# Attention over token means: the sums from ScalarE's accumulator and a row spread from DRAM instead of matrix products, with earlier weighing of the adjacency

## What is computed

```python
fea = jnp.transpose(x, (0, 2, 1))
c_adj = jnp.mean(fea, axis=1)                       # one mean for each token
diff = c_adj[:, None, :] - c_adj[:, :, None]
A = jnp.abs(jnp.abs(jax.nn.sigmoid(diff) - 0.5) - 0.5) * 2.0
A_s = (A + jnp.transpose(A, (0, 2, 1))) * 0.5
Wg = adj[None, :, :] * A_s
g = jnp.einsum('bcn,bnm->bcm', fea, Wg)
g = jax.nn.relu(g * para.reshape(1, C, N))          # the queries, 4 heads
kv = (x @ kv_w)                                     # keys and values
attn = softmax(q k^T * scale); out = attn v         # for each head
x = layernorm(x + out)
```

## Time and profile before

| | |
|---|---|
| median of 3 runs | 3213.74 us (3212.96 to 3216.64) |
| profiled execution | 3214.61 us |
| its span, first to last instruction | 3212.8 us |
| mean granted TensorE clock | 0.968 of full speed |
| busy in the span | TensorE 2929.7, VectorE 2127.5, ScalarE 1674.4, GpSimd 1066.9 us |

### The profile page before, as it was taken

The page is one execution under the profiler, slowest core; times in us unless marked ns, Lnnn a source line. Parts: engine busy times, 40 slices in busy tenths (PEclk is TensorE's granted clock), DMA queues, the critical chain, the costliest instruction groups (busy, mean ns, idle before and its releaser), DMA issues. The chain is left out here.

```text
span 3212.8 us, 38926 instructions
## 1 busy us (share of the span) xinstructions
PE 2929.7 (91%) x12436; PEld 1861.4 (58%) x12436; DVE 2127.5 (66%) x3015; ACT 1674.4 (52%) x1940; POOL 1066.9 (33%) x500
## 2 busy tenths in 40 slices
PE   6999999999999999999999999999779999988963
PEld 5454555555455554545455554545368888876853
DVE  6677777777677777767777776777353333337877
ACT  5465564646556464656656464654332222226768
POOL 1535344353635345263534435353420000000012
PEclk9999999999999999999999999999889999998976
DMA  4031211213021221303121121302122323226548
GB/s 132 20 119 40 78 59 59 74 44 118 25 93 55 63 65 52 99 22 114 50 68 59 59 83 35 118 26 66 50 88 92 105 79 117 78 92 216 190 157 280
DMA packets 168269, 276.13 MB, mean 86 GB/s; under 512 B 9760, under 2 KB 109088, under 8 KB 168224
## 3 DMA queue, kind: packets, MB, share of 16 engines
q1 hardware_dynamic: 168224, 275.55, 26.9%
HBM read 174.60 MB, written 67.11 MB: 75 GB/s over the span
## 5 line engine op out<-in xcount | busy, mean ns | idle before, releaser
L261 POOL TENSOR_TENSOR psum<-psum,probs 128x1024 f32<-128x1024 f32 x320 | 820.5, 2564 | 213.4 <-ACT probs L326 203.9
L326 ACT ACTIVATE probs<-sc_ps 128x1024 f32<-128x1024 f32 x512 | 523.3, 1024 | 648.7 <-PE sc_ps L793 648.1
L504 DVE TENSOR_REDUCE mx<-mx_ps 128x1 f32<-128x512 f32 x768 | 492.9, 684 | 168.0 <-PE mx_ps L761 162.1
L809 PE MATMUL pv_ps<-probs,v 128*64 128x512 f32 x2048 | 549.9, 615 | 2.8 <-ACT probs L326 2.6
L793 PE MATMUL sc_ps<-qa,ka 128*128 128x512 f32 x1024 | 441.1, 439 | 0.0
L793 PE MATMUL sc_ps<-qb,kb 128*128 128x512 f32 x1024 | 401.6, 397 | 0.0
L261 POOL TENSOR_TENSOR psum<-probs 128x1024 f32<-128x1024 f32 x64 | 152.7, 2386 | 695.3 <-ACT probs L326 378.0
L793 PEld LDWEIGHTS sc_ps<-qa,ka 128*128 128x128 f32 x1024 | 195.9, 193 | 260.8 <-issue 140.4
L761 PE MATMUL mx_ps<-ka,qa 128*128 128x512 f32 x768 | 299.2, 442 | 18.0 <-DVE xT_lo L458 6.4
L761 PEld LDWEIGHTS mx_ps<-ka,qa 128*128 128x128 f32 x768 | 135.3, 188 | 220.8 <-DVE mx L504 140.5
L723 PE MATMUL sc_ps<-w_hi,x_hi 128*128 128x512 f32 x512 | 211.0, 412 | 44.1 <-DVE w_lo L471 44.1
(11 more groups left out here) (182 smaller groups left out, 5285.1 us busy)
## 6 DMA issues: line engine op xcount, KB each, us to landing
adj_ring<-in_adj_dram SPq DMA_DIRECT2D x128, 512.0 KB, 3.8
pre_scratch<-pre SPq DMA_DIRECT2D x32, 1024.0 KB, 4.2
hid<-pre_scratch SPq DMA_DIRECT2D x32, 1024.0 KB, 5.0
x<-in_x_dram SPq DMA_DIRECT2D x16, 1024.0 KB, 7.4
kb<-ka SPq DMA_DIRECT2D x64, 256.0 KB, 3.1
qa<-qa SPq DMA_DIRECT2D x64, 256.0 KB, 3.3
res<-in_x_dram SPq DMA_DIRECT2D x16, 1024.0 KB, 5.6
x_scratch<-res SPq DMA_DIRECT2D x16, 1024.0 KB, 4.3
```

The costliest lines, as they stand in the source:

```text
L261: pool.tensor_tensor(psum[:, :], probs[:, 0, :] if k == 1 else psum[:, :], probs[:, k % PR, :], ALU.add).then_inc(s["pool_added"], 1)
L326: nc.scalar.activation(probs[:, i % PR, :], sc_ps[:, t % 2, :], ACT.Exp, scale=SCALE)\
L504: nc.vector.tensor_reduce(mx2[:, nh, n:n + 1], mx_ps[:, nh, :], AX.X, ALU.max)\
L809: ins = nc.tensor.matmul(pv_ps[nh * HD:(nh + 1) * HD, h % 2, :], v[:, i, h * HD:(h + 1) * HD], probs[:, i % PR, nh * BANK:(nh + 1) * BANK] ...
```

## The change

The sums over the channels come from the accumulator of the ScalarE copies that make `x_hi`, now 8 copies of a 128x256 tile instead of 2 of 128x1024, two after each of four exponentials of head 1. SyncE writes the sums to a scratch tensor in DRAM and reads it back as a row spread over all partitions, into `cb`. The factor 1/256 moves into the scale of the tanh. For this, tokens are laid out so that partition p holds tokens 8p to 8p + 7, in x and in the rows of `adj`, and x is read in one piece for each partition. `broadcast_means`, `mean_rows`, `sum_channels` and `mean_columns` are gone. `split_x` moves from the end of head 2 to the end of head 1, one `q_low` from the end of head 1 to the end of head 0, three tiles are weighed in head 2 and two more in head 3, and with them `w_high` and `w_low` move up.

```diff
+            def spread_sums(b):
+                wait(sp, s["xhi_done"], T * (b + 1))
+                sp.dma_start(sums_v, csum[:, :]).then_inc(s["sums_out"], 16)
+                wait(sp, s["sums_out"], 16 * (b + 1))
+                wait(sp, s["abs_done"], 8 * b)
+                sp.dma_start(cb[:, :], sums_row).then_inc(s["cb_in"], 16)
...
-                for h in range(1, HEADS):
-                    store_row(b, h)
+                store_row(b, 1)
                 if not last:
+                    spread_sums(b + 1)
+                store_row(b, 2)
+                if not last:
+                    load_adj(b + 1, 2)
+                store_row(b, 3)
+                if not last:
+                    load_adj(b + 1, 3)
                     copy_kb(b + 1, 0)
                     copy_kb(b + 1, 1)
-                    load_adj(b + 1, 2)
-                    load_adj(b + 1, 3)
+                    load_adj(b + 1, 4)
...
-            def x_high(b):
+            def x_high(b, tiles):
                 wait(act, s["x_in"], 16 * (b + 1))
                 wait(act, s["g_step"], 8 * b)
-                for half in range(2):
-                    tiles = slice(half * T // 2, (half + 1) * T // 2)
-                    nc.scalar.activation(x_hi[:, tiles, :], x32[:, tiles, :], ACT.Copy).then_inc(s["xhi_done"], 1)
+                wait(act, s["sums_out"], 16 * b)
+                for n in tiles:
+                    nc.scalar.activation(x_hi[:, n, :], x32[:, n, :], ACT.Copy, accum_out=csum[:, n:n + 1])\
+                        .then_inc(s["xhi_done"], 1)
...
+                q_low(b, 2)
...
                     add_head(b, h - 1)
+                    if h == 2 and not last:
+                        weigh(b + 1, 0)
                     maxima(b, h + 1, range(6, T))
                     maxima_row(b, h + 1)
                     if h == 1:
-                        q_low(b, 2)
                         q_low(b, 3)
                         if not last:
                             xt_low(b + 1, 1)
+                            split_x(b + 1)
                     if h == 2 and not last:
-                        sum_channels(b + 1)
-                        mean_columns(b + 1)
-                        split_x(b + 1)
+                        weigh(b + 1, 1)
+                        weigh(b + 1, 2)
...
                 if (h, i) == (1, 7):
                     transpose_x(b, 1)
-                if (h, i) == (2, 7):
-                    broadcast_means(b)
```

More of the change, by code:

```diff
@@ L51, in row_moments, with attention_layer @@
     nc.vector.tensor_scalar(veps, part[:, 2, :], 0.25, EPS, ALU.mult, ALU.add).then_inc(veps_done, 1)
-def attention_layer(nc, x, adj, para, kv_w, x1):
+def attention_layer(nc, x, adj, para, kv_w, sums, x1):
     B, N, C = x.shape
@@ L183, in body @@
                     load_x(b + 1)
-                for n in range(4, T):
+                for n in range(5, T):
                     load_adj(b, n)
@@ L359, in prepare @@
                     xt_high(b, 0)
-                if (h, i) == (1, 3):
-                    x_high(b)
+                if h == 1 and 2 <= i < 6:
+                    x_high(b, range(2 * i - 4, 2 * i - 2))
                 if (h, i) == (1, 7):
                     xt_high(b, 1)
-                if (h, i) == (2, 7):
-                    mean_rows(b)
+                if h == 2 and 2 <= i < 5:
+                    distance(b, i - 2)
+                    tanh_half(b, i - 2)
                 if (h, i) == (3, 0):
-                    distance(b, 0)
-                    tanh_half(b, 0)
+                    w_high(b, 0)
                 if (h, i) == (3, 1):
-                    distance(b, 1)
-                    tanh_half(b, 1)
+                    w_high(b, 1)
                 if (h, i) == (3, 2):
@@ L391, in body @@
                     head_copy(b - 1, HEADS - 1)
[L392 to L398, removed]
+                distance(b, 5)
+                tanh_half(b, 5)
+                w_high(b, 3)
+                if before:
+                    den_copy(b - 1, HEADS - 1)
+                w_high(b, 4)
+                distance(b, 6)
+                tanh_half(b, 6)
+                w_high(b, 5)
+                distance(b, 7)
+                tanh_half(b, 7)
+                w_high(b, 6)
+                w_high(b, 7)
                 q_high(b, 0)
@@ L671, in transpose_x @@
                 ins.then_inc(s["xt_ready"], 1)
-            def broadcast_means(b):
-                wait(pe, s["xtl_done"], 2 * b + 2)
-                wait(pe, s["row_done"], 4 * b)
-                for nh in range(NH):
-                    cols = slice(nh * BANK, (nh + 1) * BANK)
-                    ins = product(mx_ps[:, nh, :], [(mean_w[:, :], t[:, c, cols]) for c in range(CT)
-                                                    for t in (xT_hi, xT_lo)])
-                ins.then_inc(s["cb_ready"], 1)
             def k_product(b, c, halves=range(NH)):
                 if c == 0:
-                    wait(pe, s["cb_done"], b + 1)
+                    wait(pe, s["xtl_done"], 2 * b + 2)
+                    wait(pe, s["row_done"], 4 * b)
                 else:
```

104 lines of the change are left out of this document (42 added, 62 removed).

## The result

| | before | changed |
|---|---|---|
| median | 3213.56 us (3212.96 to 3216.64, 4 runs) | 3176.38 us (3174.78 to 3179.83, 4 runs) |
| ratio | | 0.9884, 95% interval 0.9867 to 0.9901 |
| span of the profiled execution | 3212.8 us | 3173.9 us |
| mean granted TensorE clock | 0.968 | 0.963 |

The account below looks back on a forecast made before the run. TensorE was taken as the bound, without slack. Per boundary -1.9 - 3.6 + 1.15 + 1.3 + 3.3 + 1.4 = +1.65 us; 15 of them +25 on 3214 gave 3239 us, range 3180 to 3263.

Parts of the forecast that it names:

- weigh(0) in head 2: Between `add_head` and the last two tiles of maxima, GpSimd's addition holds up the weighing; TensorE loses 3.3 us per boundary.
- products removed: Eight mean products, ending where the values of head 2 begin, leave TensorE's path: -1.9 us per boundary.
- stalls of g: In product g at a batch boundary, three TensorE stalls totalling 4.1 us shrink to about 0.5: -3.6 us per boundary.
- `q_low(2)` in head 0: Behind `xT_lo`, ahead of `add_last` and the first maxima, it has no slack: +1.15 us per boundary.
- `split_x` in head 1: Between `xT_lo` and the maxima, it makes the first maximum late for TensorE: +1.3 us per boundary.
- clock: A new 2.9 us TensorE standstill drops its granted clock four times in five: +1.4 us per boundary, bounds 0 and 1.7.
- the forecast case: weigh(0) in head 2 is blocked by GpSimd and TensorE's clock falls: 3239 us, own range 3225 to 3255, chance 0.48.
- weigh(0) is not blocked: Rival: in head 2 VectorE comes before GpSimd or a shift parts them; -1.95 us per boundary, 3185 us, chance 0.2.
- the waits pile up: Rival: late row not absorbed, its standstill drops the clock, g gains only 2.6; +73, 3287, a third 3263; chance 0.15.
- The new transfers: SyncE's sums delay the row of head 2, TensorE's wait being absorbed by one for the maximum: 0, above at 0.5.
- ScalarE: Extra accumulator reads and copies in head 1, and `distance` and `tanh` pairs in head 2, fit idle time: 0.
- The maxima have slack that I misread: Rival: TensorE's waits for the maxima have slack, leaving 1 us of losses; -5 us per boundary, 3139 us, chance 0.05.

Follow-up runs that it names:

- the means alone: Changed kernel with the weighing order, `q_low(2)` and `split_x` put back in their old places, so only the new means remain: 3187.59 us, ratio 0.9921.

## Why the prediction was wrong

The step that failed is *weigh(0) in head 2*, "I take 3.3: the starts differ by 0.05 us in GpSimd's favour in each of ten boundaries". The starts were read rightly and came out as read. Wrong was what I made of them: that the engine with the earlier recorded start has the port. What the runs showed in its place is a weighing of 1.22 us, an addition of 3.48, and a cost of 1.1 us and not 3.3. I took the rule from the earlier trace rows, where the weighing stands behind a reciprocal; here it stands behind `add_head`. The Trainium skill ("SBUF — State Buffer", Practical consequences) says that issue order, not the shape of the operation, decides who blocks. I cited it for the rival. The trace shows recorded starts and not the order of issue, and taken as a rule for two recorded starts it would have forecast the blocked side here too, which the trace does not bear out.

Each term, in us a boundary:

| term | forecast | measured | from the stretches |
|---|---|---|---|
| products removed | -1.9 | -1.84 | 9.35 against 11.19; put back, 26 / 15 |
| stalls of g | -3.6 | -4.6 | -2.85 and -1.96, without the clock's share of 0.2 |
| `q_low(2)` in head 0 | +1.15 | +1.00 | 7.42 against 6.42 |
| `split_x` in head 1 | +1.3 | +1.12 | 8.49 against 7.37 |
| `weigh(0)` | +3.3 | +1.1 | 17.99 against 16.88 with it out of the place |
| clock | +1.4 | +0.8 | +1.0 in head 2, -0.2 in head 0 |
| sum | +1.65 | -2.4 | the period fell by 2.45 |

The failed step makes 2.2 of the 4.1 us between the two sums. The second error is in g: its recorded stalls fell from 6.5 to 2.9 us, by 3.6 as forecast, but the two stretches fell by 1 us more. What that one is, I did not trace. The third is the clock. I had hung its term on the standstill of 2.9 us before the last maxima, which did not occur; the +0.8 that did come stand in the same head but come with `q_low` and `split_x`, for which I had counted no clock. What a lost us of clock costs differs by place: of the kernels that leave g and head 2 as they are, the row stored first and the products put back lose 1.46 and 0.61 us in the stretch of head 2, and it takes 18.27 and 17.47, nearly all of it; in the stretch to the end of head 0 they lose 0.24 and 1.34, and it takes 56.77 and 57.12, a third of it.

Where a memset or a wait brought the forecast case about, TensorE stood 2.64 us, the lost clock rose by 1.9 a boundary, and the kernels took 3227 us, 12 below the forecast. That case was sized about rightly, but it is not the one that happens.

The rival *weigh(0) is not blocked* is what happened, with the right size (1.1) and a time of 3185, 9 over the measured one. Its own reason, that VectorE comes first or a shift parts the two, is not in the trace: nothing shifted, and the recorded starts say that GpSimd is first. That this rival's time came so near is partly luck, too: it left out 0.8 of clock and 1.0 of gain in g, which nearly cancel. In the rival *the waits pile up*, 3263 is not the third of it that I named; 3214 + 49 takes in two thirds of the 73. The start brought 5.4 us where I took 0, but the first batch lost 5.7, and I did not trace why it gained nothing while the last batch did.

*The new transfers* at 0 held: TensorE waited for the late row in one batch (1.5 us), ahead of a maximum that was late anyway, and storing the row first changed nothing. My figure for the sums' store, 2.7 us, was too high, it is 1.4 as a rule. *ScalarE* at 0 held: in the changed kernel, ns least, median and most,

```profile
L362 ACT ACTIVATE x_hi<-x x128: 402/408/419, 13.7 to 2073.1; 128x256 fp32r<-128x256 f32 x128
L362 ACT ACTIVATION_READ_ACCUMULATOR x_hi<-x x128: 188/193/196, 14.0 to 2073.4; 128x1 f32 x128
```

*The maxima have slack that I misread* fell: there is none, since putting VectorE's work elsewhere won 61 us.

## What to carry to other kernels

Before you put a VectorE operation that reads two tiles from SBUF beside a GpSimd one, do not forecast from two recorded starts which of them is held up: cost both sides, and read it afterwards from the two lengths. The outcome of one place does not carry over to another, and an order that wins by some hundredths of a us is fragile: one harmless instruction of 0.06 us turned 1.2% faster into 0.4% slower. And where TensorE waits for VectorE, VectorE's idle gaps are the place for its side work: the same three instructions, moved to such places, made 1.2% into 3.1%.

## What the runs showed of the hardware

- VectorE kept the port over up to three small instructions and a weighing, for 1.5 us (3.88 - 2.38) in which GpSimd's addition stood. Between two full-size ones, 128x1024, GpSimd got in although they followed without a gap, 15 of 15. What makes the difference was not tried.
- `add_head`, with one operand in PSUM and one in SBUF, neither waits for the port nor holds it: 0.27 us for each instruction beside an addition that has the port and alone, and an addition that starts while it runs takes its 2.37 to 2.40 where maxima follow.
- Recorded starts do not tell who has the port. The recorded length holds the waiting: GpSimd's was 3.47 to 3.90 us instead of 2.38 here, VectorE's 3.28 to 3.43 instead of 1.22 on the losing side.
- The same small store took 1.4 us at the median and 3.2 at most; the one boundary that I had looked at closely was the exception.
- The granted clock falls to 0.50 (1.2 GHz) for 3.4 us at a time, 1.7 us of work each; in the three kernels with a memset or a wait ahead of `weigh(0)` some falls last 6.8 us. Between 150 and 2150 us 17.1 us were lost before, 22.2 after, 8.5 with the means alone and 49.4 with the memset of 128x64. It does not follow the standstills alone: with `weigh(0)` out of the place TensorE stood less and 30.7 us were lost.
